# Norm roots by a GpSimd power, the infinities' step by comparisons, and a new order of work in a two-layer decoder kernel

## The reference

```python
x = x + self_attention(ln(x))            # norm 0: 16 heads, causal; keys, queries, values by one matrix
x = x + cross_attention(ln(x), ctx)      # norm 1
x = x + moe(ln(x))                       # norm 2: 8 experts and a shared one, top 2, silu
x = x + state_space(ln(x))               # norm 3
x = x + masked_cross_attention(ln(x), ctx, mask)   # norm 4: 8 heads
x = x + expert_choice(ln(x))             # norm 5: 8 experts, gelu

def state_space(x):                      # states: s = s @ A.T + B x, over 64 steps; y = C s
    act = gelu(y)
    norm = (act - mean(act)) / sqrt(var(act) + 1e-5) * gamma + beta
    return nan_to_num(norm, nan=0.0, posinf=1e6, neginf=-1e6)
```

## Time and profile before

| What | Value |
|---|---|
| Time, median of 3 runs (lowest to highest) | 286.17 us (282.66 to 288.06) |
| The profiled execution's own time | 284.46 us |
| Its span, first to last instruction | 282.1 us |
| TensorE busy, mean granted clock | 260.9 us (92%), 0.954 |
| VectorE busy, instructions | 205.0 us (73%), 730 |
| ScalarE busy | 148.1 us (53%) |
| GpSimd busy | 69.5 us (25%) |
| Chain that ended last: TensorE, VectorE, ScalarE | 79%, 14%, 3% |
| VectorE's norms (L1619): 48 tiles | 13.5 us, 346 ns each |

### The profile page before, as it was taken

One profiled execution on the slowest core, in us unless ns is written; L12 is line 12 of the kernel. 1 busy time (PEld: TensorE's weight loads), 2 busy tenths in 40 slices (PEclk: granted clock), 3 DMA queues, 4 the chain that ended last, 5 costly groups with the idle time before them and its releaser, 6 DMA issues.

```text
span 282.1 us, 5322 instructions
## 1 busy us (share of the span) xinstructions
PE 260.9 (92%) x1836; PEld 177.6 (63%) x1836; DVE 205.0 (73%) x730; ACT 148.1 (53%) x307; POOL 69.5 (25%) x124
## 2 busy tenths in 40 slices
PE   8999999988989999999989648899999999999993
PEld 8645689567744665675673313468877456767783
DVE  4567987899767748476329969977677488889964
ACT  1567566354344683985863433285644854444541
POOL 5453993000000424565770000044410000000000
PEclk9999999999897999999995985899999999999998
DMA  5599900218203000000000000000000000000002
GB/s 138 131 270 263 272 12 2 37 37 242 59 14 63 1 0 2 1 1 0 2 1 0 0 1 0 2 2 2 3 2 3 0 0 2 1 0 2 0 0 74
DMA packets 22038, 11.62 MB, mean 41 GB/s; under 512 B 11016, under 2 KB 21005, under 8 KB 22013
## 3 DMA queue, kind: packets, MB, share of 16 engines
q1 hardware_dynamic: 21117, 11.01, 14.7%
q0 software_dynamic: 80, 0.20, 0.7%
q10 hardware_dynamic: 816, 0.10, 0.2%
HBM read 8.68 MB, written 2.62 MB: 40 GB/s over the span
## 4 chain that ended last, share of the span: by engine, by line
PE 79%; DVE 14%; ACT 3%; issue 2%; DVEq 0%; ACTq 0%
PE bank L908 10%; PE bank L896 9%; PE bank L761 6%; PE bank L767 6%; PE bank L786 6%; PE bank L645 4%; PE bank L566 3%; PE bank L534 3%; PE bank L666 3%; PE bank L569 3%; PE bank L843 2%; PE bank L881 2%; PE bank L586 2%; PE bank L652 2%; PE bank L804 2%
## 5 line engine op out<-in xcount | busy, mean ns | idle before, releaser
L496 POOL TENSOR_TENSOR X<-X,att 128x128 f32<-128x128 f32 x72 | 30.2, 454 | 72.5 <-ACT att L1333 72.3
L908 PEld LDWEIGHTS bank<-Wb,att 128*128 128x128 f32 x256 | 29.7, 192 | 3.0 <-ACT att L1373 1.5
L908 PE MATMUL bank<-Wb,att 128*128 128x128 f32 x256 | 30.8, 277 | 0.7 <-ACT att L1373 0.7
L896 PE MATMUL bank<-XT,Wb 128*128 128x512 f32 x64 | 30.2, 601 | 0.0
L1795 DVE SCALAR_TENSOR_TENSOR att<-bank,cols,att 128x512 f32<-128x512 f32 x18 | 13.5, 750 | 15.1 <-ACT att L1322 7.0
L1373 ACT ACTIVATE att<-bank 128x512 f32<-128x512 f32 x32 | 18.8, 600 | 9.6 <-PE bank L896 9.6
L1333 ACT ACTIVATE att<-bank,comb 128x128 f32<-128x128 f32 x72 | 20.1, 378 | 5.7 <-PE bank L786 5.5
L786 PEld LDWEIGHTS bank<-W2a,att 128*128 128x128 f32 x144 | 17.9, 192 | 4.3 <-issue 4.0
L1933 DVE SCALAR_TENSOR_TENSOR X<-big,rt,X 128x128 f32<-128x128 f32 x64 | 17.7, 347 | 3.9 <-ACT big L1381 3.7
L509 POOL TENSOR_TENSOR Es<-Es,sm 128x512 f32<-128x512 f32 x8 | 8.3, 1042 | 49.0 <-DVE sm L1857 49.0
L1381 ACT ACTIVATE big<-bank 128x512 f32<-128x512 f32 x16 | 9.6, 598 | 19.5 <-PE bank L908 19.5
(11 more groups left out here) (235 smaller groups left out, 528.8 us busy)
## 6 DMA issues: line engine op xcount, KB each, us to landing
Wb<-in_L_ffn_W SPq DMA_DIRECT2D x1, 1024.0 KB, 5.5
Wb<-in_L_ffn_W SPq DMA_DIRECT2D x8, 128.0 KB, 5.2
X<-in_x SPq DMA_DIRECT2D x2, 256.0 KB, 3.3
k_scratch<-QKVT SPq DMA_DIRECT2D x1, 512.0 KB, 3.1
q_scratch<-QKVT SPq DMA_DIRECT2D x1, 512.0 KB, 2.9
Wb<-k_scratch SPq DMA_DIRECT2D x1, 512.0 KB, 4.4
v_scratch<-QKVT SPq DMA_DIRECT2D x1, 512.0 KB, 5.4
V<-q_scratch SPq DMA_DIRECT2D x1, 512.0 KB, 6.3
```

The costliest lines, as they stand in the source:

```text
L496: nc.gpsimd.tensor_tensor(X[:, h * HT + t, :], X[:, h * HT + t, :], part0[:, i % 2, t, :], ALU.add).then_inc(f_acc, 1)
L896: mm(bank[i % 4][:, :], W1b[:, e, f * P:(f + 1) * P], XT[:, half(h)], start=True, stop=True).then_inc(m_up, 1)
L908: last = mm(bank[4 + h][:, t * P:(t + 1) * P], hid[:, e % 2, f, tile], W2b[:, e, f, :], start=(f == 0), stop=(f == F1 - 1))
```

## The change

Three things change together.

1. **The root goes to GpSimd.** VectorE keeps var + eps (now at the end of `ln_moments` and `states_moments`) and raises l_var; GpSimd raises the four numbers to the power -0.5 (`root`, a tensor_tensor with a tile of -0.5) and raises l_root, for which `ln_apply` and `states_apply` wait. Norm 0's root is two now. GpSimd's list is written out and has the 14 roots in it.
2. **The states.** They are scaled by gamma ahead of their root (`states_scale`: (GA - mean) * gamma), and then multiplied by the root and increased by beta in one step a tile. The infinities are found by comparison with the largest fp32 number: GpSimd takes 1e6 off X where the value was minus infinity (`subtract_low`), VectorE makes 1e6 where it was plus infinity, finds the finite ones, puts them back and adds. Five steps of VectorE in place of six; GpSimd has one.
3. **Orders and semaphores.** The lists of TensorE, ScalarE and VectorE are put in another order, and some load semaphores are joined, so that a few waits ask for more loads than before.

```diff
@@ semaphores joined
-            sp.dma_start(Wk1[:, :], w["L1_xattn_W_k"]).then_inc(ld_kv1, 16)
-            sp.dma_start(Wv1[:, :], w["L1_xattn_W_v"]).then_inc(ld_kv1, 16)
+            sp.dma_start(Wk1[:, :], w["L1_xattn_W_k"]).then_inc(ld_x0, 16)
+            sp.dma_start(Wv1[:, :], w["L1_xattn_W_v"]).then_inc(ld_x0, 16)
...
-            sp.dma_start(Wq1[:, :], w["L1_xattn_W_q"]).then_inc(ld_x1, 16)
+            sp.dma_start(Wq1[:, :], w["L1_xattn_W_q"]).then_inc(ld_rows, 16)
...
             def keys0(h):
-                pe.wait_ge(ld_x0, 48)
+                pe.wait_ge(ld_x0, 80)
...
-            act.wait_ge(c_azero, 1)
+            act.wait_ge(c_zero, 3)
@@ gpsimd
+            def root(k, h):
+                cut = tiles(h)
+                pool.wait_ge(l_var[h], k + 1)
+                nc.gpsimd.tensor_tensor(rs[:, 0, cut], rs[:, 1, cut], halves[:, :], ALU.pow).then_inc(l_root[h], 1)
...
+            nc.gpsimd.memset(halves[:, :], -0.5).then_inc(c_zero, 1)
...
             nc.gpsimd.memset(causal[:, :, :], 0.0).then_inc(c_fill, 1)
 
+            pool.wait_ge(c_zero, 2)
+            root(0, 0)
+            root(0, 1)
             pool.wait_ge(xn_ready[1], HT)
...
+            def subtract_low(h):
+                cut = tiles(h)
+                pool.wait_ge(s_gelu[h], 2)
+                nc.gpsimd.tensor_tensor(X[:, cut, :], X[:, cut, :], low[:, cut, :], ALU.subtract).then_inc(s_low[h], 1)
...
+            root(1, 0)
+            root(2, 0)
+            root(1, 1)
+            add_part(0, 0, 0)
...
+            add_part(0, 3, 0)
+            root(2, 1)
+            add_part(0, 3, 1)
...
+            add_part(1, 0, 3)
+            root(3, 0)
+            add_part(1, 1, 0)
...
+            root(3, 1)
+            root(4, 0)
+            subtract_low(0)
+            root(5, 0)
+            root(4, 1)
+            subtract_low(1)
+            root(5, 1)
             weigh_probs(0)
...
             weigh_probs(7)
+            root(6, 0)
+            root(6, 1)
@@ vector
             def ln_moments(n, h):
...
                 moments(X, h)
+                cut = tiles(h)
+                V.tensor_scalar(rs[:, 1, cut], mv[:, cut, 1], EPS, None, ALU.add).then_inc(l_var[h], 1)
 
             def ln_apply(n, h):
+                dve.wait_ge(l_root[h], n + 1 if n < 4 else n + 2)
...
+            def states_scale(h):
+                dve.wait_ge(ld_rows, 96)
+                for t in range(h * HT, (h + 1) * HT):
+                    last = V.scalar_tensor_tensor(GB[:, t, :], GA[:, t, :], mv[:, t, 0:1], gamma[:, :], ALU.subtract,
+                                                  ALU.mult)
+                then(last)
 
             def states_apply(h):
+                dve.wait_ge(l_root[h], 5)
                 for t in range(h * HT, (h + 1) * HT):
-                    last = V.tensor_scalar(GB[:, t, :], GA[:, t, :], mv[:, t, 0:1], rs[:, 0, t:t + 1], ALU.subtract,
-                                           ALU.mult)
+                    last = V.scalar_tensor_tensor(GB[:, t, :], GB[:, t, :], rs[:, 0, t:t + 1], beta[:, :], ALU.mult,
+                                                  ALU.add)
                 then(last)
...
                 if step == 0:
-                    then(V.tensor_tensor(mask, gb, gb, ALU.is_equal))
+                    V.tensor_scalar(low[:, cut, :], gb, -FMAX, CLAMP, ALU.is_lt, ALU.mult).then_inc(s_gelu[h], 1)
                 if step == 1:
-                    then(V.tensor_scalar(ga, gb, CLAMP, -CLAMP, ALU.min, ALU.max))
+                    then(V.tensor_scalar(ga, gb, FMAX, CLAMP, ALU.is_gt, ALU.mult))
                 if step == 2:
-                    then(V.tensor_tensor(ga, ga, mask, ALU.mult))
+                    then(V.tensor_scalar(mask, gb, 0.0, 0.0, ALU.mult, ALU.is_equal))
                 if step == 3:
-                    then(V.tensor_scalar(mask, gb, 0.0, 0.0, ALU.mult, ALU.is_equal))
+                    then(V.copy_predicated(ga, mask, gb))
                 if step == 4:
-                    then(V.copy_predicated(ga, mask, gb))
-                if step == 5:
+                    dve.wait_ge(s_low[h], 1)
                     then(V.tensor_tensor(X[:, cut, :], ga, X[:, cut, :], ALU.add))
@@ vector's order, norm 1 and the states (the roots' calls go everywhere)
-            mask_row()
             outputs_by_feature(0)
...
             normalise(8)
+            normalise(9)
             add_attention(0)
             ln_moments(1, 0)
-            root_guess(0)
-            normalise(9)
-            root_third(0)
-            root_second(0)
+            subtract_max(13)
             ln_apply(1, 0)
...
             ln_apply(2, 0)
+            mask_row()
             gate_sub(0)
...
             ln_moments(4, 0)
-            root_guess(0)
             states_moments(1)
-            root_guess(1)
-            root_third(0)
-            root_second(0)
             ln_apply(4, 0)
-            root_third(1)
-            root_second(1)
+            states_scale(1)
             states_apply(1)
-            affine_states(1)
...
             ln_moments(5, 0)
-            root_guess(0)
-            root_third(0)
-            root_second(0)
+            add1(4)
             ln_apply(5, 0)
-            add1(4)
@@ tensor's order: keys_values1(13) now ahead of inject(1), (14) where (13) was,
@@ and (15) behind the transposes of norm 4, half 0
             transpose_xn(3, 1, 6)
+            keys_values1(13)
             inject(1)
             widen(1, 0)
             widen(1, 1)
-            keys_values1(13)
+            keys_values1(14)
             widen(1, 2)
...
-            keys_values1(14)
             read_out(1)
+            transpose_xn(4, 0, 0)
             keys_values1(15)
-            transpose_xn(4, 0, 0)
```

More of the change, by code:

```diff
@@ new lines, in _ @@
+            add_part(0, 5, 2)
+            add_part(0, 5, 3)
+            add_part(0, 6, 0)
+            add_part(0, 6, 1)
+            add_part(0, 6, 2)
+            add_part(0, 6, 3)
+            add_part(0, 7, 0)
+            add_part(0, 7, 1)
+            add_part(0, 7, 2)
+            add_part(0, 7, 3)
+            add_part(0, 8, 0)
+            add_part(0, 8, 1)
+            add_part(0, 8, 2)
+            add_part(0, 8, 3)
+            add_part(1, 0, 0)
+            add_part(1, 0, 1)
+            add_part(1, 0, 2)
@@ new lines, in _ @@
+            add_part(1, 4, 3)
+            add_part(1, 5, 0)
+            add_part(1, 5, 1)
+            add_part(1, 5, 2)
+            add_part(1, 5, 3)
+            add_part(1, 6, 0)
+            add_part(1, 6, 1)
+            add_part(1, 6, 2)
+            add_part(1, 6, 3)
+            add_part(1, 7, 0)
+            add_part(1, 7, 1)
+            add_part(1, 7, 2)
+            add_part(1, 7, 3)
+            add_part(1, 8, 0)
+            add_part(1, 8, 1)
+            add_part(1, 8, 2)
+            add_part(1, 8, 3)
@@ L1819, in affine_states @@
-            def affine_states(h):
-                cut = tiles(h)
-                dve.wait_ge(ld_rows, 64)
-                then(V.tensor_tensor(GB[:, cut, :], GB[:, cut, :], per_col(gamma[:, :], HT), ALU.mult))
-                then(V.tensor_tensor(GB[:, cut, :], GB[:, cut, :], per_col(beta[:, :], HT), ALU.add))
             def add_states(h, step):
                 cut = tiles(h)
-                ga, gb, mask = GA[:, cut, :], GB[:, cut, :], nanm[:, cut, :]
+                ga, gb, mask = GA[:, cut, :], GB[:, cut, :], finm[:, cut, :]
@@ L2103, in _ @@
             subtract_max1(6)
+            add1(0)
             subtract_max1(7)
```

366 lines of the change are left out of this document (169 added, 197 removed).

## The result

The changed kernel takes 275.17 us in the median of four runs (274.64 to 277.64), the kernel before 285.64 in the four runs beside it (282.66 to 288.06): a ratio of 0.9732, interval 0.9682 to 0.9783. The forecast was 278.5 us. The profiled execution of the changed kernel took 274.64 us, its span is 272.7 us against 282.1, so 9.4 us are to be found between two traces for which my sum said 6.0.

What follows compares the result with a forecast made beforehand. TensorE (busy 260.9 of 282.1 us) leaves room only where it idles, waits or runs at half clock. Gains 0.3 + 1.4 + 0.8 + 2.3 + 1.2 = 6.0 off the profiled 284.46 us gave 278.5, range 273.5 to 283.5.

Steps and rivals of the forecast that it cites:

- norm 1: Half 0, an unbroken VectorE chain: eight steps go and a subtract_max covers the exchange with GpSimd, gain 1.4 us.
- norm 2: Half 0: nothing covers the exchange with GpSimd, so the root's move saves 1.6 - 0.8 = 0.8 us.
- norm 5: Half 1, ending in TensorE's route(1): last additions 0.8 us earlier, exchange gives 0.8 more, route(1) about 1.2 earlier: 1.2 us.
- its own mechanism: VectorE's shorter chains give the summed gains: likeliest 278.5 us, own range 276 to 281, chance 0.43.
- The power: GpSimd's root on four elements: 0.6 us, between 0.26 and 1.9, plus 0.1 for each hand-over.
- States and norm 4: Between read-out and first maximum of attention 1: VectorE 5 us earlier, TensorE later, so 2.3 us arrive (1.5 to 4.3).
- with the clock back as long after the restart as before: At norm 4's queries: TensorE's full clock returns 7.8 us after restart, at 175.7 us, so scores 0 end at 178.9.
- Rival (a): Full clock stays at the queries (+2.0 us) and at 85.7 to 89 (1.6): 274.9 us, chance 0.20.
- The costs put at nothing: Wider waits, add_bias and the probabilities' scaling queued behind a root, and new orders in full TensorE stretches: each 0.
- Widened waits: keys0, the queries of attention 1 and ScalarE's first DMA issue wait for more loads or a memset: together 0.
- The first power: At norm 0, a slow first power loses what exceeds 3.4 us of slack; with 6 us, 281.1 us; chance 0.04.
- the start: Norm 0 gains 0.1 us, and VectorE's earlier bv add and fourth key block 0.2: together 0.3, between 0 and 1.

Runs made afterwards that it cites:

- The second execution: The kernel before, unchanged, run and traced once more: measured 285.11 us, span 283.3 us, mean clock 0.954.
- the holding matmuls: The kernel before with 16 matmuls into an unused bank in TensorE's gap ahead of norm 4: 282.33 us, ratio 0.9890; once more for a trace, 285.13 us.

## Why the forecast was right, and where not

Between the two profiled executions, in the order of the span, each piece measured between two events that both traces have (the half-clock stretches known from them are given apart):

| Piece | forecast | measured | of it clock |
|---|---|---|---|
| to the first add of attention 0 (60.67, 61.12) | 0.3 | -0.45 | |
| to the applications of norm 1, half 0 | 1.4 | 1.2 | |
| to the applications of norm 2, half 0 (81.32, 79.06) | 0.8 | 1.5 | 0.9 |
| to the states' statistics, half 1 (165.50, 159.82) | 0 | 3.4 | 3.0 |
| to the first maximum of attention 1 | 2.3 | 3.3 | |
| to the statistics of norm 5, half 0 (206.47, 197.89) | 0 | -0.4 | |
| to route(1) (219.91, 210.62) | 1.2 | 0.7 | |
| to the end | 0 | 0.1 | |
| sum | 6.0 | 9.4 | 3.9 |

The 0.9 is the difference of the two executions of the kernel before over that piece. The 3.0 is an estimate: 3.3 us of full work at 0.50 from 85.7 (1.65 lost) that after does not have, and 6.2 us from 147.2 (3.1 lost) against 3.5 from 143.5 to 147 (1.75 lost).

The measured 275.17 us lie inside the stated range of 273.5 to 283.5, but outside the 276 to 281 that the forecast kept for its own mechanism. Without the clock 5.5 us are left in this pair, and 6.7 by all executions at equal clock; the forecast of 6.0 lies between them. **The mechanism was right in kind**: the gains are those of VectorE's chains at norm 1, norm 2, norm 4 and norm 5 of the halves named, with the full stretches unchanged. The sizes were less good: 1.2 for 1.4, 0.6 for 0.8, 3.3 for 2.3, 0.7 for 1.2 and -0.45 for 0.3. That they add up to nearly my sum is in part luck.

**The power** was sized at 0.6 and measures 1.02. That makes an open root worth 0.5 instead of 0.8, and can take about 0.3 of the 0.5 that norm 5 lacks; the rest there has no cause shown. My reason, that four elements must be near the low end of a line through 128 and 512, was sound for a multiplication (0.21 measured) and not for another function.

**States and norm 4** is the mis-sized term, 2.3 for 3.3. I had VectorE's side nearly right (ready 11.1 us after the statistics began; 12.2 measured, of which 0.94 is GpSimd's subtraction, which I had named as 1.0 but left out of my sum). What failed is TensorE's side: *with the clock back as long after the restart as before*, 7.8 us. The clock came back 4.9 us after the restart (162.4 to 167.3), so from the transposes to the end of scores 0 TensorE needed 9.8 us (162.40 to 172.21) and not the 11.0 that I gave it, and the two engines met within 0.2 us (VectorE's last application ends at 172.03). That I held TensorE to be the bound there made me count VectorE's 5 us at half.

**What I left out** is the other clock. Rival (a), *the clock holds*, gave 274.9 us and the result is 275.17, but by other places than it named. It counted 2.0 us at the queries. There the clock did fall. A full clock is worth nothing there before (15.76 us with it, 15.75 without) and 0.3 us after (12.13 against 12.44), where a longer fall costs 0.6 (13.06). Its 1.6 at 85.7 did come, and 1.4 at 147 and 0.9 at 75 besides, which no case of mine had. I read the four half-clock stretches of one execution as properties of the program. The second execution shows that three of them are not there every time: they are a cost spread over the whole kernel, and between one pair of traces part of it can look like a gain of the change. By mean clock (0.961 in 37 executions before, 0.977 in four after) that share is 1.6 x 1.53 = 2.4 us.

Why the mean clock is higher after is not settled. The kernels with both the new roots and the new states' steps have 0.969 to 0.983, those with one of them or neither 0.957 to 0.962; with the holding matmuls three of five executions of the kernel before had 0.982 and two 0.961 and 0.968. In the kernel before, TensorE had idled a little ahead of each of the first three falls (busy for 0.92 of 1.4 us from 74.0, 1.37 of 2.0 from 82, 0.47 of 1.2 from 146). But the second execution runs the same program without these falls, so such a gap is not enough by itself, and no run takes the gaps away one by one.

**The costs put at nothing** held with one exception. Widened waits, add_bias, the probabilities behind the last root: the table of waits of the kernel after has none on any of them. The first power took 1.02 us like the others. The Trainium skill, GPSIMD Engine Reference, "2.1 Instruction dispatch", has about 6 us for a first call into freshly loaded code; nothing of that kind is seen at the first power here. The exception is the start, 0.45 us later instead of 0.3 earlier; two executions of the same kernel differ there by 3.2 us, so I give it no cause. And the new orders cost about 5 us without the short roots, and are perhaps worth 2 with them, which is not clear of the noise; of these 0.6 lies at the first maximum (12.44 against 13.08). I had put them at 0 in the full stretches and folded them into the other terms elsewhere.

## What to carry to other kernels

An order of instructions fits the durations that it was chosen for: the new order without the new roots cost 5 us here, and with them about 2 us may have been won, so an order is costed together with the durations. Take TensorE's half-clock stretches from several executions before you put one of them into a sum at its place; at one place ask first whether TensorE sets that stretch at all. A function on four elements on GpSimd has a price of its own that a line through additions does not give.

## What the hardware showed that I had not expected

- A GpSimd power costs 1.02 us on four elements and 0.74 on two, a multiplication on four 0.21, and the first power is no dearer than the others.
- VectorE's four-element steps take 0.38 us instead of 0.16 to 0.17 while GpSimd adds beside them, and start 0.41 us apart instead of 0.20: nine of them 3.45 us instead of 1.79. A comparison of 128x512 takes 1.37 us instead of 0.43 beside a GpSimd subtraction.
- Of two executions of one program, one had a clock of 0.50 at 75.4, 85.7 and 147.2 us and the other had 1.00 there and 0.51 from 158 to 179.
- With TensorE given work in one gap, its clock was 1.00 through the queries in two traces, and in both it fell in a later stretch (177.5 to 184.5, 179.5 to 187), where the kernels without that work had 1.00 in their traces. That the one caused the other is not shown: the kernel with the new orders alone has no such work, and its clock fell inside attention 1 too, between 186 and 194 us.
